# The second attention turns its operands by DMA transposes instead of on TensorE

## The reference

```python
q = rms_norm((draft @ Wq.T).reshape(.., 16, 128), q_norm_w)      # 16 query heads
kv_in = concatenate([context, draft], axis=1)                    # 128 + 128 tokens
k = rms_norm((kv_in @ Wk.T).reshape(.., 4, 128), k_norm_w)       # 4 key heads
v = (kv_in @ Wv.T).reshape(.., 4, 128)
q, k = rope(q, pos_q), rope(k, pos_kv)                           # x*cos + rotate_half(x)*sin
scores = einsum('bhqd,bhkd->bhqk', q, repeat(k, 4)) / sqrt(128)
attn = einsum('bhqk,bhkd->bhqd', softmax(scores), repeat(v, 4))
x = x + attn.reshape(.., 2048) @ Wo.T                            # draft = layernorm(x)
```

## Time and profile before

| | |
|---|---|
| median of 3 runs | 3359.56 us (3355.34 to 3360.89) |
| the profiled execution, its own time | 3357.83 us |
| its span, first to last instruction | 3356.0 us |
| the second attention, first input load to last result | 2064 to 2903 us |
| mean granted TensorE clock over the span | 0.948 |

### The profile page before, as it was taken

The page is one execution under the profiler, slowest core; times in us unless marked ns, Lnnn a source line. Parts: engine busy times, 40 slices in busy tenths (PEclk is TensorE's granted clock), DMA queues, the critical chain, the costliest instruction groups (busy, mean ns, idle before and its releaser), DMA issues. The chain is left out here.

```text
span 3356.0 us, 58815 instructions
## 1 busy us (share of the span) xinstructions
PE 2983.1 (89%) x17284; PEld 1767.7 (53%) x17285; DVE 1847.9 (55%) x5780; ACT 1650.6 (49%) x4374; POOL 1684.7 (50%) x2331
## 2 busy tenths in 40 slices
PE   4699999999999789999999995999999999734996
PEld 2366666666666545555555542555555555422663
DVE  4366666656665564434443363778878877421331
ACT  5577777777777533332333242555555555311332
POOL 6477667766776345534544453544444444241222
PEclk8799999999999989999999997999999999856998
DMA  7601101110110155544554473000000000217444
GB/s 239 216 30 42 38 28 35 41 38 28 35 44 29 67 178 156 152 134 138 154 155 140 129 221 68 17 26 19 19 25 19 19 25 14 65 74 273 85 83 105
DMA packets 202977, 285.48 MB, mean 85 GB/s; under 512 B 38721, under 2 KB 109633, under 8 KB 202817
## 3 DMA queue, kind: packets, MB, share of 16 engines
q1 hardware_dynamic: 140016, 204.89, 18.8%
q0 software_dynamic: 16640, 38.05, 5.6%
q10 hardware_dynamic: 46224, 41.36, 4.2%
HBM read 194.95 MB, written 93.50 MB: 86 GB/s over the span
## 5 line engine op out<-in xcount | busy, mean ns | idle before, releaser
L437 PE MATMUL a_mm<-a_w_hi,a_xq_hi 128*128 128x512 f16 x768 | 298.4, 389 | 64.0 <-POOL a_xq_lo L885 60.9
L601 DVE BATCH_NORM_STATS2 a_st<-a_mm 128x6 f32<-128x128 f32 x768 | 170.8, 285 | 318.8 <-PE a_mm L438 225.3
L750 ACT ACTIVATE a_nrm<-a_mm,a_sc_t 128x128 f32<-128x128 f32 x768 | 290.5, 473 | 105.9 <-POOL a_sc_t L903 105.7
L1646 POOL TENSOR_TENSOR e_st<-e_st,e_ws_tile 128x1024 f32<-128x1024 f32 x64 | 124.5, 1946 | 428.3 <-PE e_y L1402 417.5
L438 PE MATMUL a_mm<-a_w_hi,a_xq_lo 128*128 128x512 f16 x768 | 298.4, 389 | 0.0
L1535 DVE SCALAR_TENSOR_TENSOR e_hl<-e_ha,e_hh 128x512 f16<-128x512 f32 x128 | 88.5, 691 | 352.0 <-ACT e_hh L1440 351.6
L1440 ACT ACTIVATE e_hh<-e_ha 128x512 f16<-128x512 f32 x128 | 76.3, 596 | 415.3 <-PE e_ha L1387 413.7
L902 POOL TENSOR_TENSOR a_sc_t<-a_sc_t,a_mhalf 128x4 f32<-128x4 f32 x192 | 199.9, 1041 | 133.1 <-DVE a_sc_t L608 132.7
L1401 PE MATMUL e_y<-e_w2l,e_hh 128*128 128x512 f16 x640 | 242.9, 380 | 0.0
L1402 PE MATMUL e_y<-e_w2h,e_hl 128*128 128x512 f16 x640 | 242.9, 380 | 0.0
L1400 PE MATMUL e_y<-e_w2h,e_hh 128*128 128x512 f16 x640 | 242.9, 380 | 0.0
(11 more groups left out here) (357 smaller groups left out, 8653.7 us busy)
## 6 DMA issues: line engine op xcount, KB each, us to landing
e_st<-in_w SPq DMA_DIRECT2D x128, 512.0 KB, 4.1
disp<-a_empty SPq DMA_DIRECT2D x16, 781.5 KB, 4.1
e_st<-in_w1b SPq DMA_DIRECT2D x32, 352.0 KB, 3.1
e_xb<-disp ACTq DMA_DIRECT2D x41, 260.5 KB, 2.7
disp<-a_empty SPq DMA_DIRECT2D x4, 2605.0 KB, 21.5
e_xb<-disp SPq DMA_DIRECT2D x40, 260.5 KB, 4.3
a_cx<-in_ctxT SPq DMA_DIRECT2D x32, 256.0 KB, 3.1
a_stage<-in_wprojT SPq DMA_DIRECT2D x16, 512.0 KB, 5.0
```

The lines of the kernel that those rows point to most:

```text
L437: pe.matmul(out, xq_hi[:, n, c, :], w_hi[:, t, c, :], start=(c == 0), stop=False)
L750: ins = act.activation(nrm[:, n % 2, i * P:(i + 1) * P], src[:, i * P:(i + 1) * P], ACT.Identity, bias=sc_t[:, n % 2, 3, i:i + 1], scale=s ...
```

## The change

No transpose is left on TensorE in this stage. The halves are made first, in the untransposed layout and in SBUF, and SP issues one DMA transpose for each half: `x_turn` (2 for each batch, 128x512 fp16), `q_turn` (12, 128x512), `p_turn` (8, 128x1024). `QTB` and `PTB` are gone. ScalarE's `q_high` moves to the slot of `normalise`, `x_high` to that of `x_norm`; `p_high` now scales four 128x256 pieces by the reciprocal row sums, and `p_low` does scaling and subtraction in four instructions, which takes the place of `pnorm` and of the two subtractions. VectorE's `bn_aggr` goes: GpSimd combines mean and spread of the even and odd elements itself (six small instructions instead of five). The attention scale and the 1/WS factor are folded into the norm weights once at the start (two more GpSimd instructions there), so the product with -SCALE goes; `r2` is made by one instruction with a reversed access pattern instead of two.

```diff
+            def p_turn(b, a, q):
+                for half, done in ((0, "phi"), (1, "plo")):
+                    sp.wait_ge(sem[done], at(a, NA1, b))
+                    if half == 0:
+                        sp.wait_ge(sem["pv"], at(a - 2, NA1, b) + 2)
+                    sp.sem_inc(sem["turning"], 1)
+                    sp.dma_start_transpose(pT[half][:, a % 2, :, :].rearrange("p c (i t) -> p (c i) t", t=P),
+                                           pq[half][:, a % 2, :, :, :].rearrange("p c i t -> p (c i t)"))\
+                      .then_inc(turned[half][a % 2], 16)
...
+            def q_turn(b, t, q):
...
+                for half, done in ((0, "qhi"), (1, "qlo")):
+                    sp.wait_ge(sem[done], at(n, NN1, b))
+                    sp.sem_inc(sem["turning"], 1)
...
+                    out = kT[half][:, q, :, n, :] if n < 2 else qT[half][:, n - 2, :].rearrange("p (i t) -> p i t", t=P)
+                    sp.dma_start_transpose(out, nq[half][:, n % 2, :]).then_inc(q_turned[half][n % 2], 16)
 
-            run_pipeline(sp, [("end", 7, store), ("end", 2, residual), ("in", 1, x_load)],
+            run_pipeline(sp, [("in", 5, x_turn), ("job", 2, q_turn), ("att", 3, p_turn), ("end", 7, store), ("end", 2, residual), ("in", 1, x_load)],
                          NJ1, SCORE1, None, 2)
...
             def scores(b, a, q):
-                pe.wait_ge(sem["qlo"], at(2 + a, NN1, b))
+                for half in range(2):
+                    pe.wait_ge(q_turned[half][a % 2], 16 * at(a // 2 + 1, NN1 // 2, b))
...
             def pv(b, a, q):
                 pe.wait_ge(sem["vlo"], at(1, NV1, b))
-                pe.wait_ge(sem["plo"], at(2 * a + 1, 2 * NA1, b) + 1)
+                for half in range(2):
+                    pe.wait_ge(turned[half][a % 2], 16 * at(a // 2, NA1 // 2, b))
...
-            run_pipeline(pe, [("job", 0, project), ("job", 2, q_transpose), ("in", 5, x_transpose), ("att", 0, scores),
-                              ("att", 5, pv), ("att", 6, out_project),
-                              ("att", 2, lambda b, a, q: p_transpose(b, a, 0)),
-                              ("att", 3, lambda b, a, q: p_transpose(b, a, 1))], NJ1, SCORE1, None, 2)
+            run_pipeline(pe, [("job", 0, project), ("att", 0, scores),
+                              ("att", 5, pv), ("att", 6, out_project)], NJ1, SCORE1, None, 2)
...
+            def p_low(b, a, q):
+                dve.wait_ge(sem["phi"], at(a, NA1, b))
+                if not is0(b, a, 2):
+                    dve.wait_ge(turned[1][a % 2], 16 * at(a // 2 - 1, NA1 // 2, b))
                 for i in range(4):
...
+                    ins = dve.scalar_tensor_tensor(out=pq[1][:, a % 2, :, i, :],
+                                                   in0=pr[:, a % 2, i, :].rearrange("p (c t) -> p c t", c=2),
+                                                   scalar=ri[:, a % 2, i:i + 1], in1=pq[0][:, a % 2, :, i, :],
+                                                   op0=ALU.mult, op1=ALU.subtract)
...
-            run_pipeline(dve, [("job", 3, q_low), ("in", 6, x_low), ("att", 1, smax),
-                               ("att", 3, lambda b, a, q: p_low(b, a, 0)), ("att", 4, lambda b, a, q: p_low(b, a, 1)),
-                               ("att", 2, pnorm), ("job", 0, stats), ("job", 1, v_low), ("att", 5, o_low),
+            run_pipeline(dve, [("job", 2, q_low), ("in", 5, x_low), ("att", 1, smax),
+                               ("att", 3, p_low), ("att", 2, row_scale), ("job", 0, stats), ("job", 1, v_low), ("att", 5, o_low),
                                ("end", 7, final), ("in", 3, x_stats)], NJ1, SCORE1, ch, 2)
```

More of the change, by code:

```diff
@@ new lines, in x_turn @@
+            def x_turn(b, k, q):
+                for half, done in ((0, "x_hi"), (1, "x_lo")):
+                    sp.wait_ge(sem[done], b + 1)
+                    sp.sem_inc(sem["turning"], 1)
+                    if half == 0 and not (isinstance(b, int) and b < 2):
+                        sp.wait_ge(sem["mm"], at(NJ1 - 1, NJ1, b - 2))
+                        sp.sem_inc(sem["turning"], 1)
+                    sp.dma_start_transpose((src_hi, src_lo)[half][:, q, 1, :, :], xq[half][:]).then_inc(x_turned[half], 16)
@@ L1800, in project @@
                 mm.then_inc(sem["mm"], 1)
[L1802 to L1814, removed]
             def scores(b, a, q):
-                pe.wait_ge(sem["qlo"], at(2 + a, NN1, b))
+                for half in range(2):
+                    pe.wait_ge(q_turned[half][a % 2], 16 * at(a // 2 + 1, NN1 // 2, b))
+                    if a == 0:
+                        pe.wait_ge(q_turned[half][1], 16 * at(0, NN1 // 2, b))
                 if not is0(b, a, 1):
@@ L1873, in x_low @@
                 dve.wait_ge(sem["x_hi"], b + 1)
[L1874 to L1876 removed]
+                if not is0(b):
+                    dve.wait_ge(x_turned[1], 16 * b)
+                dve.tensor_tensor(xq[1][:], xn[:], xq[0][:], ALU.subtract).then_inc(sem["x_lo"], 1)
             def v_low(b, t, q):
@@ L1895, in stats @@
                 for i in range(4):
-                    ch.add(dve.bn_stats(st[:, n, i, :], src[:, i * P:(i + 1) * P]))
-                ch.wait()
-                for i in range(4):
-                    ins = dve.bn_aggr(mv[:, n, i, :], st[:, n, i, :])
+                    ins = dve.bn_stats(st[:, n, i, :, :].rearrange("p o s -> p (o s)"), src[:, i * P:(i + 1) * P])
                     ch.add(ins) if i < 3 else ins.then_inc(sem["stat"], 1)
@@ L1915, in q_low @@
                 dve.wait_ge(sem["qhi"], at(n, NN1, b))
-                src = QTB[:]
-                if n < 2:
-                    hi, lo = (k[:, q, :, n, :] for k in kT)
-                    src = QTB[:].rearrange("p (h t) -> p h t", h=4)
-                else:
-                    hi, lo = (x[:, n - 2, :] for x in qT)
-                dve.tensor_tensor(lo, src, hi, ALU.subtract).then_inc(sem["qlo"], 1)
+                if not is0(b, n, 2):
+                    dve.wait_ge(q_turned[1][n % 2], 16 * at(n // 2 - 1, NN1 // 2, b))
```

168 lines of the change are left out of this document (81 added, 87 removed).

## The result

The changed kernel takes 3307.19 us (median, 3304.89 to 3308.09), the kernel before 3357.45 in the same comparison: ratio 0.9849, 95% interval 0.9832 to 0.9866, or 1.5% faster. The prediction was 3234 us, a gain of 126 us where 50 came.

A forecast was written before the change was run, and what follows sets the result against it. TensorE was taken as the bound; 8.4 us less in each of 15 batches, 126 us, gave 3357.8 - 126 + 1.7 = 3234 us, 3.7% faster. The range was 3214 to 3465 us, the forecast's own region 3214 to 3255.

The forecast's parts named there:

- The bound before: TensorE bounds the stage: 48.3 us of products and transposes in a 50.25 us batch, 1.5 us of QTB waits.
- TensorE's part: All 15 transpose groups (6.7 us), QTB waits (1.5) and half the unnamed 0.45 go: 8.4 us a batch, 126 in all.
- The turns: 22 DMA transposes a batch on SP's queue: a mean turn costs 0.6 to 1.2 us, TensorE waits only beyond 1.8.
- the range's slow end: Whole program: 3465 us, set to take in rivals 2, 5 and most of rival 3.
- Rival 3: SP's queue: transposes go one at a time, each until landed; 55.8 us a batch, +84 us, 3442; chance 0.17.
- Rival 4: DMA transposes go block by block, 120 blocks at 2.1 us: 252 us a batch, +3000, 6390 us; chance 0.05.
- Both are covered by TensorE: ScalarE at 29.5 of 41.6 us, GpSimd at 23.4 plus under 2, show only if they hold up a chain.
- the paragraph on latency: Turned halves reach TensorE in time: 11 us needed of 13, 2 us to spare; exponentials end about with their slot.
- the last clause of the prediction: Sign of being wrong: TensorE waits for a projection's bank, which would put the cause on VectorE; no size given.
- the 38 that the prediction allowed as its worst: VectorE's work a batch: about 34 us, 38 if reversed pattern and two SBUF operands cost half as much again.
- GpSimd's chain: On GpSimd, one tiny instruction more for each of six jobs cannot cost 2 us; covered by TensorE.
- Rival 2: Mean turn about 2.0 us, or VectorE's late halves hold up scores: 45.6 us a batch, 3288 us; chance 0.13.

The follow-up runs named there:

- e9: Kernel before with only the shorter statistics, rotation and folded factor, every transpose staying on TensorE; 3354.84 us, ratio 0.9989.
- e14: Changed kernel with VectorE's maximum, 1/sum and late probabilities ahead of q_low and x_low, one small GpSimd instruction folded away, addition in two signalled halves; 3243.41 us.
- e1: Changed kernel with p_low working on one of its four heads only, the other late probabilities left zero; 3314.08 us.
- e13: Changed kernel with GpSimd's addition on 16 of 128 columns of each head, nothing added beside it, tables kept; 3245.02 us.
- e17: Changed kernel with GpSimd's addition on 16 of 128 columns, led by three linked products of four columns to keep the chain's length; 3290.53 us.

## Why the prediction was half right

- **The bound before** was right: taking 4 us a batch from VectorE alone (e9) gave 4 us in all.
- **TensorE's part** was right: all 15 groups and the QTB waits are gone. Its own work is 41.65 us a batch (e14), 41.6 forecast.
- **The turns** were right, and the range's slow end was not needed. SP's timeline has an issue of 1.20 us for a turn of 128x512 and 1.27 for one of 128x1024, and the page's DMA issues (count, median us to landing) read:

```profile
2231.12 1.27 SPq L1770 DMA_TRANSPOSE a_pl<-a_pql  x1
...
2233.69 1.20 SPq L1797 DMA_TRANSPOSE a_qh<-a_nqh  x1
2234.99 1.20 SPq L1797 DMA_TRANSPOSE a_ql<-a_nql  x1
```

```profile
a_qh<-a_nqh SPq DMA_TRANSPOSE x64, 2.4
...
a_ph<-a_pqh SPq DMA_TRANSPOSE x64, 3.2
```

  Rival 3 (one at a time, each until it has landed) falls: the last turn above is issued 1.30 us behind the one before it, which takes 2.4 to land, and 14 x 2.4 + 8 x 3.2 = 59 us of landing are done in 46.8. Rival 4 (block by block) falls too: a turn of 128x1024, eight blocks, lands in 3.2 us. The DMA engines' own work was a little more than forecast: a share of 0.51 of 46.8 us, less the 0.07 of 50.25 before, is 20 us for the turns where 17 was estimated. The Trainium skill, page "VectorE: DVE Perf Modes", section "The three transpose paths", gives 1309 ns for one block; by adding that up a turn would take 10.5 us, an estimate from that page, and no row here shows that.
- **The step that failed** is the sentence on ScalarE and GpSimd, "Both are covered by TensorE, and would show only if they held up a chain (below)", together with the paragraph on latency, which was to check those chains. It followed the turned halves and the scores, and found 2 us to spare; it never followed the projection's bank, nor asked what stands behind each waiting instruction on ScalarE and VectorE. With TensorE's 50 us a batch that ring had room. At 41.9 it had not: 46.8 us is the ring's time. The mechanism is in the words of the last clause of the prediction ("if it waits for a projection's bank"), with VectorE named as the cause; but e1 shows that it isn't VectorE's amount of work: 5.2 us a batch less of it gave nothing. Of the 62 us between the changed kernel and e13, some 39 go with the chain's length and some 23 with the addition's traffic.
- **Mis-sized terms:** p_low 2.3 us a group instead of 1.05 (1.66 with GpSimd idle; what else stretches it is not taken apart), with which VectorE came to 39.3 us a batch, above the 38 that the prediction allowed as its worst; the other halves from SBUF up to 1.7 instead of 0.6; GpSimd's chain from 3.60 to 4.01 us, taken as nothing, is by e13's and e17's price some 18 us (argued from that price, not run by itself); TensorE's slow matmuls behind gaps 1.3 us a batch, priced only in rival 3.
- **Rival 2** gave 3288 us and is nearest in size, by the wrong place: mean turns are 1.2 us, and turned queries held up nothing. Two sums are a little off and change nothing: rival 4's 3357.8 + 3026 is 6384, not 6390, and the chances of a faster time add up to 0.75, not 0.74.
- **Open:** how the 5 us a batch divide exactly between order, chain and stretch; the runs price each in one direction only (order 21 us, chain 44 us per us, stretch 23), and they overlap. No run shortens ScalarE's part of the ring, so its price is unknown.

## What to carry to other kernels

When the bound engine's work is cut, compare the next bound not only with each engine's busy time but with the ring of hand-overs between in-order queues: for each instruction that waits, write down what is queued behind it and who waits for that. Here its length counted, not its load: a small instruction off GpSimd's serial chain, or a result signalled in two halves, gave more (23 and 20 us) than three quarters of VectorE's late probabilities (nothing). Before moving an operand from PSUM to SBUF, look at what GpSimd runs beside it.

## What the runs showed of the hardware

- A VectorE instruction of 128x512 with both operands in SBUF takes 0.69 us alone and 1.72 when GpSimd's addition of 128x512 has just begun; with one operand in PSUM it keeps 0.67 even then. An instruction of 128x4 on SBUF took 1.03 instead of 0.17. GpSimd pays too: its addition took 1.54 when VectorE's subtraction had begun 0.27 us before it (2220.49 above), 1.26 otherwise, and its mean went from 1266 to 1374 ns.
- A fused scale-and-subtract of four pieces of 128x256 in SBUF takes 1.66 us on VectorE with GpSimd idle; the four scalings before took 1.14.
- 30 DMA transposes a batch of 47 us from one queue, at a DMA share of 0.75, held up nobody; issuing one takes 1.2 us of SP's time, against 0.35 for a plain load, and several are on their way at once (59 us of landing in 46.8).
- The granted clock fell to 0.50 after a gap of 2.07 us, and not in the gap (1.00) but 0.9 us after its end.
